# Graph layer on one Trainium2 core: the third kind's 256 edges multiplied directly in float32, a gather ring of eight slots, two of three tiles gathered plainly

## What is computed

```python
h = relu(layernorm(x))
feat = concat([h[src], h[dst]], axis=1)                 # 8192 x 2048
e_hh = relu(feat[:256] @ W_hh + b_hh)
e_oo = relu(feat[256:1536] @ W_oo + b_oo)
e_ho = relu(feat[1536:] @ W_ho + b_ho)
logit = concat([e_hh, e_oo, e_ho]) @ W_a + b_a          # one number per edge
alpha = softmax of logit over the edges of each dst
z = segment_sum(alpha[:, None] * h[src], dst)
x = x + relu([h, z] @ W_hn or W_on + bias)              # rows 0..127 W_hn, the others W_on
out = x + (normalised adjacency) @ (relu(layernorm(x)) @ W1.T + b1)
```

## Time and profile before

| | |
|---|---|
| median of 3 runs | 615.08 us |
| the profiled execution's own time | 616.7 us |
| its span in the profile | 614.9 us |
| TensorE busy | 559.2 us (91%) |
| VectorE busy | 446.3 us (73%) |
| ScalarE busy | 295.0 us (48%) |
| GpSimd busy | 183.1 us (30%) |
| DMA | 144.71 MB, mean 235 GB/s |

### The profile page before, as it was taken

The page is one execution under the profiler, slowest core; times in us unless marked ns, Lnnn a source line. Parts: engine busy times, 40 slices in busy tenths (PEclk is TensorE's granted clock), DMA queues, the critical chain, the costliest instruction groups (busy, mean ns, idle before and its releaser), DMA issues.

```text
span 614.9 us, 8170 instructions
## 1 busy us (share of the span) xinstructions
PE 559.2 (91%) x2360; PEld 409.3 (67%) x2361; DVE 446.3 (73%) x948; ACT 295.0 (48%) x471; POOL 183.1 (30%) x177
## 2 busy tenths in 40 slices
PE   1799999999796998898989987997998999999997
PEld 1688777777463676655657665564656887878885
DVE  6729157579596897899999967969547558888352
ACT  0723311122218989674857354958664445225200
POOL 3002110066355456445765466242000100000000
PEclk9899999999887999999998998789997899999999
DMA  8448774389999899999999999886864537502121
GB/s 324 156 148 287 245 266 154 110 194 374 346 310 319 268 322 313 341 290 331 373 354 345 304 334 336 271 216 166 284 214 128 191 92 250 186 0 86 52 86 51
DMA packets 56550, 144.71 MB, mean 235 GB/s; under 512 B 6338, under 2 KB 6466, under 8 KB 56514
## 3 DMA queue, kind: packets, MB, share of 16 engines
q0 software_dynamic: 22352, 81.28, 42.9%
q1 hardware_dynamic: 27072, 50.34, 24.2%
q10 hardware_dynamic: 7090, 12.65, 5.5%
HBM read 125.37 MB, written 18.87 MB: 235 GB/s over the span
## 4 chain that ended last, share of the span: by engine, by line
PE 47%; DVE 21%; DMA 15%; ACT 6%; issue 6%; POOL 3%; ACTq 1%; DVEq 0%; POOLq 0%
PE ps L710 29%; DMA gath<-tab_b,tabl_i 10%; PE ps L660 4%; PE ps L842 4%; PE ps L895 4%; DVE ring_l L970 4%; DVE gath L995 3%; ACT onehot L530 3%; PE ps L873 3%; DVE gath L990 2%; DMA gath<-tab_a,tabl_i 2%; DVE onehot L1011 2%; DMA tab_b<-stage 1%; DVE stage L978 1%; POOL gath L339 1%
## 5 line engine op out<-in xcount | busy, mean ns | idle before, releaser
L710 PE MATMUL ps<-ring_h,actT_h 128*128 128x512 f32 x504 | 218.9, 434 | 5.7 <-DVE actT_l L965 3.1
L710 PE MATMUL ps<-ring_h,actT_l 128*128 128x512 f32 x504 | 201.1, 399 | 0.0
L710 PE MATMUL ps<-ring_l,actT_h 128*128 128x512 f32 x504 | 200.8, 398 | 0.0
L530 ACT ACTIVATE onehot<-onehot,lgs 128x512 bf16<-128x512 bf16 x192 | 123.5, 712 | 64.1 <-DVE onehot L1011 57.5
L477 ACT CAST ring_h<-raw 128x512 fp32r<-128x512 f32 x160 | 94.9, 618 | 91.0 <-PE ps L710 68.7
L970 DVE TENSOR_TENSOR ring_l<-raw,ring_h 128x512 fp32r<-128x512 f32 x160 | 107.5, 687 | 27.0 <-ACT ring_h L477 26.6
L710 PEld LDWEIGHTS ps<-ring_h,actT_h 128*128 128x128 f32 x504 | 97.3, 193 | 38.8 <-DVE actT_l L965 3.3
L710 PEld LDWEIGHTS ps<-ring_h,actT_l 128*128 128x128 f32 x504 | 97.2, 193 | 22.0
L710 PEld LDWEIGHTS ps<-ring_l,actT_h 128*128 128x128 f32 x504 | 97.5, 193 | 19.9
L660 PE MATMUL ps<-onehot 128*128 128x512 bf16 x292 | 82.4, 393 | 27.1 <-ACT onehot L530 20.1
L995 DVE SCALAR_TENSOR_TENSOR gath<-gath,wa_b 128x1024 f32<-128x1024 f32 x64 | 78.4, 1225 | 27.6 <-DMA gath<-tab_b,tabl_i 25.6
(11 more groups left out here) (182 smaller groups left out, 539.2 us busy)
## 6 DMA issues: line engine op xcount, KB each, us to landing
raw<-in_L_gnn_W_ho_dram SPq DMA_DIRECT2D x32, 256.0 KB
raw<-in_L_gnn_W_oo_dram SPq DMA_DIRECT2D x32, 256.0 KB
raw<-in_L_gnn_W_hh_dram SPq DMA_DIRECT2D x32, 256.0 KB
raw<-in_L_gnn_W_on_dram SPq DMA_DIRECT2D x32, 256.0 KB
raw<-in_L_gnn_W_hn_dram SPq DMA_DIRECT2D x32, 256.0 KB
tab_a<-stage ACTq DMA_DIRECT2D x24, 256.0 KB
tab_b<-stage ACTq DMA_DIRECT2D x24, 256.0 KB
raw<-in_L_gnn_W_dram SPq DMA_DIRECT2D x16, 256.0 KB
```

The costliest lines, as they stand in the source:

```text
L530: ins = nc.scalar.mul(onehot[:, s, 1 + i, :], onehot[:, s, 1, :], lgs[:, i, q:q + 1])
L710: mm = nc.tensor.matmul(ps[:, first + m, :], w, v, start=(k == 0 and i == 0), stop=(k == KT - 1 and i == 2))
```

## The change

1. Kind hh gets no tables. Its 256 edges (2 tiles) are multiplied directly: GpSimd gathers the rows h[src] and h[dst] of both tiles from a stored copy `h_rows` (4 gathers), TensorE transposes them in chunk 1 (32 transposes of 128x128), ScalarE clips them at zero (8 operations), and the features of src stay in SBUF, those of dst are stored and loaded again (1 MB each way). The four hh chunks 8 to 11 become 16 float32 matmuls each, out of `raw` itself, with no rounding, no low part, no copies and no stores. VectorE adds the bias and takes the logits out of PSUM (`hh_edges`, 8 operations).
2. The ring has 8 slots in place of 10. Of the 62 tiles that are still gathered from tables, two of three are plain (41 plain, 21 accumulated); before it was 31 plain and 33 accumulated. The accumulating transfer is issued 2 tiles later in place of 3, and 5 tiles are begun ahead of `tab_b` in place of 6.
3. The order is written anew. Chunks 6 and 7 keep 7 tiles' sums each; the hh chunks have 5 sums and about 4 edges each; 12 and 13 have 7 and 5 sums. 16 of the 62 tiles and the 2 of hh are summed behind chunk 13, in two rounds "14" and "15" with no chunk under them; the first product of the node rows 0 to 127 stands among these, the second behind them. The kinds are closed in the order ho, hh, oo.
4. `inverse_counts` works on 1024 columns at a time in place of 256, and `hrow_l` is made a little earlier.

```diff
-        GB = 10
-        gath = sb("gath", [P, GB, D], F32, over="hrow", shift=8 * D)
+        GB = 8
+        gath = sb("gath", [P, GB, D], F32, over="hrow", shift=16 * D)
...
-        PLAIN = [q for q in range(T_HO + T_OO) if q % 2]
-        USES = [(q, e) for q in range(ET) for e in ((0, 1) if q in PLAIN else (0,))]
+        PLAIN = [q for q in range(TG) if q % 3]
+        USES = [(q, e) for q in range(TG) for e in ((0, 1) if q in PLAIN else (0,))]
...
+            def store_rows():
+
+                for m in range(NM):
+                    sp.wait_ge(s_norm, m + 1)
+                    sp.dma_start(h_rows[m * P:(m + 1) * P, :], hrow[:, m, :]).then_inc(s_hd, 16)
...
+            def load_behind_hh(w, row, n, c, k):
+
+                sp.wait_ge(s_slot, KT + (CH_HH + c) * KT + k + 1)
+                sp.dma_start(raw[:, k, :], w[row + k * P:row + (k + 1) * P, n * FB:(n + 1) * FB]).then_inc(s_raw[k], 16)
...
+            pool.wait_ge(s_hidx, 64)
+            pool.wait_ge(s_hd, 16 * NM)
+            for i in range(2 * T_HH):
+                pool.indirect_dma_start(out=hh_rows[:, i, :], out_offset=None, in_=h_rows[:, :],
+                                        in_offset=bass.IndirectOffsetOnAxis(ap=hh_i[:, i:i + 1], axis=0)).then_inc(s_hg[i], 16)
...
-            LAG = 3
-            FIRST = 6
+            LAG = 2
+            FIRST = 5
...
+        SUM_AT = {(6 + i, k): (i * 7 + k,) for i in range(2) for k in range(7)}
+        SUM_AT |= {(8 + i, k): (14 + i * 5 + j,) for i in range(4) for j, k in enumerate((0, 2, 3, 5, 6))}
+        SUM_AT |= {(12, k): (34 + k,) for k in range(7)}
+        SUM_AT |= {(13, k): (41 + k,) for k in range(5)}
+        SUM_AT |= {(14, 0): (46, 47), (14, 1): (48,), (14, 2): (49,), (14, 3): (50, 51), (14, 5): HH_TILES, (14, 6): (52, 53),
+                   (14, 7): (54, 55), (15, 0): (56, 57), (15, 1): (58, 59), (15, 2): (60,), (15, 3): (61,)}
...
+        EDGE_AT = {divmod(4 * KT + 4 + i // 7 * KT + i % 7, KT): (i,) for i in range(24)}
+        EDGE_AT |= {divmod(8 * KT + 2 * i, KT): (24 + i,) for i in range(16)}
+        EDGE_AT |= {(11, 7): (40,)}
+        EDGE_AT |= {divmod(12 * KT + (3 * i) // 2, KT): (41 + i,) for i in range(10)}
+        EDGE_AT |= {(14, 0): (51,), (14, 1): (52,), (14, 2): (53,), (14, 3): (54,), (14, 5): (55,), (14, 6): (56,), (14, 7): (57,),
+                    (15, 0): (58, 59), (15, 1): (60,), (15, 2): (61,)}
...
+            def hh_transposes(k):
+
+                for j in HH_AT.get(k, ()):
+                    if j == 0:
+                        for i in range(2 * T_HH):
+                            pe.wait_ge(s_hg[i], 16)
+                    if j >= 2:
+                        pe.wait_ge(s_ft, j - 1)
+                    for f in (2 * j, 2 * j + 1):
+                        for t in range(T_HH):
+                            c = f % 2 * E_HH + t * P
+                            mm = nc.tensor.transpose(ps[:, 2 + j % 2, c:c + P], hh_rows[:, 2 * t + f // KT, f % KT * P:(f % KT + 1) * P], ident[:, :])
+                    mm.then_inc(s_ftp, 1)
...
+            def hh_chunk(c):
+
+                half, n = HH[c]
+                for k in range(KT):
+                    sums(CH_HH + c, k)
+                    pe.wait_ge(s_raw[k], (CH_HH + c) * 16 + 16)
+                    if half and k == 0:
+                        pe.wait_ge(s_fld, 16)
+                    for t in range(T_HH):
+                        b = HH_BANK[n][t]
+                        if half == 0 and k == 0:
+                            pe.wait_ge(s_copied, NM * CH_HH + b - NM + 1)
+                        mm = nc.tensor.matmul(ps[:, b, :], featT[half][:, k, t * P:(t + 1) * P], raw[:, k, :],
+                                              start=(half == 0 and k == 0), stop=(half == 1 and k == KT - 1))
+                    mm.then_inc(s_slot, 1)
...
-            with pe.Fori(0, 6) as i:
-                edge_chunk(i + 6, before=lambda k: uniform_sums(i, k))
+            for q in (6, 7):
+                edge_chunk(q, before=lambda k: sums(q, k))
+            for c in range(4):
+                hh_chunk(c)
...
+            for k in range(4):
+                sums(14, k)
+            head_rows(0)
+            for c in (14, 15):
+                for k in range(4 if c == 14 else 0, KT):
+                    sums(c, k)
+            head_rows(1)
...
+            def hh_edges(n):
+
+                chunk_done(dve, CH_HH + 2 + n)
+                dve.wait_ge(s_bias, 48)
+                for t in range(T_HH):
+                    b = HH_BANK[n][t]
+                    c = slice(n * FB, (n + 1) * FB)
+                    step(nc.vector.tensor_tensor(ps[:, b, :], ps[:, b, :], bias2[:, 0, c], ALU.add))
+                    nc.vector.scalar_tensor_tensor(out=ps[:, b, :], in0=ps[:, b, :], scalar=0.0, in1=wa_b[:, c],
+                                                   op0=ALU.max, op1=ALU.mult, accum_out=lgh[:, t, n:n + 1]).then_inc(s_hhd, 1)
```

More of the change, by code:

```diff
@@ L170, in gnn_kernel @@
         s_root = sem("square_roots")
+        s_hd = sem("h_stored")
+        s_hidx = sem("hh_edges_loaded")
+        s_hg = [sem(f"hh_rows_gathered{i}") for i in range(2 * T_HH)]
+        s_ftp = sem("hh_transposed_banks")
+        s_ft = sem("hh_features_ready")
+        s_fst = sem("hh_dst_stored")
+        s_fld = sem("hh_dst_loaded")
+        s_hhd = sem("hh_banks_read")
         s_norm = sem("h_normed")
@@ L212, in gnn_kernel, with is_split, nth_split @@
         block = ctx.enter_context(nc.Block())
-        KINDS = ((W_ho, b_ho), (W_oo, b_oo), (W_hh, b_hh))
-        TILES = (T_HO, T_OO, T_HH)
-        CH_EDGE = 3 * 2 * NN
+        CH_HH = 2 * 2 * NN
+        CH_EDGE = CH_HH + 2 * NN
+        TG = T_HO + T_OO
+        HH = [(half, n) for half in range(2) for n in range(NN)]
+        HH_BANK = ((5, 6), (7, 4))
+        def is_split(q):
+            return not CH_HH <= q < CH_EDGE
+        def nth_split(q):
+            return q if q < CH_HH else q - (CH_EDGE - CH_HH)
         hn, on = (W_hn, (0,)), (W_on, (1, 2, 3))
@@ L221, in gnn_kernel @@
                 for r, order in ((0, ((on, 0), (on, 1))), (D, ((hn, 0), (hn, 1), (on, 0), (on, 1))))]
-        PLAIN = [q for q in range(T_HO + T_OO) if q % 2]
-        USES = [(q, e) for q in range(ET) for e in ((0, 1) if q in PLAIN else (0,))]
+        PLAIN = [q for q in range(TG) if q % 3]
+        USES = [(q, e) for q in range(TG) for e in ((0, 1) if q in PLAIN else (0,))]
         USE = {u: c for c, u in enumerate(USES)}
-        ADDED = {q: sum(1 for p in range(q + 1) if p not in PLAIN and USE[p, 0] % GB == USE[q, 0] % GB) for q in range(ET)}
+        ADDED = {q: sum(1 for p in range(q + 1) if p not in PLAIN and USE[p, 0] % GB == USE[q, 0] % GB) for q in range(TG)}
         def h_bank(k):
@@ L371, in _ @@
             bias(0, b_hh)
-            for q in range(FIRST, ET):
-                if q in (T_HO, T_HO + T_OO):
+            pool.wait_ge(s_ft, KT)
+            for q in range(FIRST, TG):
+                if q == T_HO:
                     tables_landed(kinds_of(q))
@@ L456, in _ @@
                     to += n
+            for e, end in enumerate((src, dst)):
+                for t in range(T_HH):
+                    act.dma_start(hh_i[:, 2 * t + e:2 * t + e + 1], end[t * P:(t + 1) * P].rearrange("(p a) -> p a", a=1)).then_inc(s_hidx, 16)
             def root(i):
@@ L570, in edge_chunk @@
                         seed(*SEED_AT[q, k])
-                    if k == 3 and 0 < q <= CH_EDGE and not is_a(q - 1):
+                    if k == 3 and 0 < q <= CH_HH and not is_a(q - 1):
                         store_b(q - 1)
@@ L588, in _ @@
             q = CH_EDGE + 2
-            keep_second_halves()
+            keep_second_halves((1,))
+            for at_ in SUM_AT:
+                if at_[0] >= q:
+                    for t in SUM_AT[at_]:
+                        logit_parts(t)
+            act.wait_ge(s_ohu, OS + 2 * ET)
+            keep_second_halves((2, 3))
             act.wait_ge(s_degin, 1)
@@ L1172, in top @@
             def top(m, n):
-                return topsum[:, m, n * FB:(n + 1) * FB] if m == 0 or n else stage[:, m - 1, :]
+                if m == 0 or m > 1 and n:
+                    return topsum[:, m, n * FB:(n + 1) * FB]
+                return stage[:, 3 if n else m - 1, :]
             def update_row(c, m):
```

257 lines of the change are left out of this document (151 added, 106 removed).

## The result

The changed kernel takes 628.7 us (median of 4, 627.7 to 634.3) against 614.9 for the kernel before beside it; the ratio is 1.025, 95% interval 1.020 to 1.031. I had said 603, with a range to 624. What came is rival B, which I had worked out at 629. The profiled execution took 628.2 us, its span is 626.4.

A forecast was written before the change was run, and what follows sets the result against it. No engine alone was taken to bound; the new ring's chain would set chunks 6 to 12. Chunk 6 to first exponential 19.4 us less, transposes 7.1 more: 616.7 - 12.3 = 604.4 profiled, 603 median, range 586 to 624.

The forecast's parts named there:

- rival B: Chunks 6 to 12 and tail: eight-slot ring too short, 5.3 us a tile, ending at 629 by the median; chance 0.20.
- start of chunk 6, against 187.2: Chunk 1: 32 added transposes at 0.222 us each on TensorE delay everything behind by 7.1 us.
- chunks 6 to 12: Logits of 36 tiles at 4.8 us each, 173 us.
- chunk 13: Goes by TensorE with four tiles only: 72 matmuls at 0.229 and five sums, 20.5 us.
- rounds 14 and 15, to the last one-hot: Behind chunk 13: 11 tiles by DMA or VectorE's work, both some 46, taken as 48 us for a float32 product.
- last one-hot to first exponential: Before the softmax: three ScalarE products 1.9, sum and closing 1.7, copies and root 4.0, together 7.6 us.
- behind the first exponential: Softmax and after: left as before; second product and loads of h's parts taken as covered.
- the pace: Chunks 6 to 12: a ring chain of 14.4 us for three tiles, 4.8 us a tile.
- L: In the ring chain: an accumulation from issue to landing, taken as 7.5 us, not the 11.58 of a full queue.
- the other links: Ring chain besides the landing: dst issue, gap, logits, add and other VectorE work, 6.9 us for three tiles.
- Rival A: Chunks 6 to 12 and tail: DMA binds, not the ring, 4.4 us a tile, 586 by the median; chance 0.22.
- Rival C: Behind chunk 13: TensorE idles, clock falls, round trip uncovered, 60 us in place of 48, total 615; chance 0.13.

The follow-up runs named there:

- before8: Kernel before with only the change's gather scheme (8 slots, two of three tiles plain, accumulation 2 tiles later, 5 begun early): 643.6 us, ratio 1.041.
- mid: Changed kernel with each accumulation issued between the src and dst gathers of a tile instead of behind both: 615.7 us, ratio 0.998.
- LAG 1: Accumulation issued one tile later: changed kernel (instead of two) 614.4 us; kernel before (instead of three) 626.1 us.
- beforelag1: Kernel before with the accumulation issued one tile later in place of three, nothing else: 626.1 us, ratio 1.019.
- half1tail: Changed kernel with every second tile plain, accumulation issued one tile later, and last sums reordered: 621.0 us, ratio 1.005.

## Why the prediction was wrong

The sum, against the profile of the changed kernel:

| term | said | measured | difference |
|---|---|---|---|
| start of chunk 6, against 187.2 | +7.1 | +1.5 | -5.6 |
| chunks 6 to 12 | 173 | 196.2 | +23.2 |
| chunk 13 | 20.5 | 21.4 | +0.9 |
| rounds 14 and 15, to the last one-hot | 48 | 49.5 | +1.5 |
| last one-hot to first exponential | 7.6 | 9.1 | +1.5 |
| behind the first exponential | 159.2 (as before) | 161.5 | +2.3 |

604.4 - 5.6 + 23.2 + 0.9 + 1.5 + 1.5 + 2.3 = 628.2, the profiled execution.

**The step that failed** is the pace, 4.8 us a tile. The mechanism was right, link for link, as before8 and mid show; two of its terms were sized too low. I took L, the accumulation from issue to landing, at 7.5 us, the lowest of two rows, "since a ring with fewer transfers out keeps the queue short". The ten accumulations on the chain between 157 and 358 us took 5.8 to 9.6, on average 8.0. And I took 6.9 us for the other links; between accumulations that follow each other on the chain there are 5.8 to 8.8 us, 7.5 on average over seven such gaps, the longer ones with another instruction of VectorE's order among them (1.1 + 1.2 us of the counts' inverses at 294.7). The seven loops that stand whole on the chain take 15.8 us for three tiles in place of 14.4, 5.26 a tile, past the point of 5.15 from which I had said it is a loss. The five in the two stretches where the chain runs over TensorE's order take 16.3 on average. What had seemed to confirm the reckoning was no check: (7 + 11.58)/4 = 4.6 took one row for the old ring, where only four accumulations of chunks 6 to 11 stand on the chain at all (10.0 to 11.6 us), at a DMA share of 0.99 to 1.03. So the old loop seldom bound, its L was no measure of the new one, and the 7.5 was chosen on an argument. Of the 23.2 us in the table some 18 are the pace, 36 tiles at 5.30 in place of 4.8; the other 5.3 are a 37th tile, which I had counted outside this stretch.

**Rival B** was therefore right in its place and in its pace (5.3 a tile), and had 0.20. That its total hit as well (630 by the profile, 628.2 came) is in part luck: it had 5.6 us too much for the transposes and 6.5 too much for the tail (56 against 49.5), and 5.2 too little for chunks 6 to 12 (191 against 196.2). **Rival A** could not be, as the loop stood above DMA's 4.4; in mid, without the loop, the pace was 4.84, so its 4.4 was not reached even then: the written order came next, with DMA at an estimated 4.65 close behind. By the Trainium skill, "DMA: Bandwidth & Descriptors", the section on the anatomy of a GpSimd-issued DMA, a landing would take an estimated 3.2 us; I gave that road to A. No accumulation on the changed kernel's chain landed in under 5.7 us, so the trace decides against it here.

**Rival C**, the naked tail, did not come. It had 60 us to the last one-hot in place of 48, and 49.5 were measured; VectorE is busy 39.3 of 53.5 us there, 73%. To the exponential there are 58.6 us against the 48 + 7.6 = 55.6 of my own sum, so the tail cost 3 us more, not 12. What it said of the clock is seen: 0.73 in that stretch. That the tail and the gathers take turns as its bound was not in any rival.

**The other signs.** Chunk 2 opens at 70.4, not 76: the transposes were another term mis-sized, in the other direction. Chunk 1 takes 3.6 us longer than before in place of 7.1; the other 2 us by which it opens early are chunk 0's, 22.0 us at a granted clock of 1.00 in this execution and 23.7 at 0.94 in that of the kernel before, and owe nothing to the change. The transposes stand in the stream of matmuls as

```profile
50.56 0.87 PE ps L879 x8
51.44 5.46 PE ps L811 x24
56.90 0.87 PE ps L879 x8
```

8 in 0.87 us, 0.109 each, 3.5 us for all 32. The row I took, 25 in 5.55 us, is of the first work TensorE does. The matmuls right behind it, from 22.93 us on in the kernel before, stand 0.43 us apart up to 25.6 and 0.23 after that, and the granted clock is 0.73 of 2.4 GHz from 20 to 25 us; so the row was probably of half speed, though the profile lists 1.00 from 10 to 20. The hh chunks took 87.4/4 = 21.9 us, above my 19 to 21; their matmuls are what I had said (in mid 8 records, four products, in 3.43 us, 0.86 each, against 0.88), so TensorE's 32 us are gained and go into the ring's pace, and without the loop the hh chunks take 20.2 each. The wait of 8.8 us for the hh tables is gone, GpSimd's waits for the logit are 148 us, where I had put B's sign at 150. The part behind the softmax I had left alone: 2.3 us more in this execution, 1.0 in mid's, not looked into.

## What to carry to other kernels

Where one engine issues a ring's transfers in a fixed order, write down behind which tile's completion and behind which landing each issue stands, and close both loops, in the old and in the new version; then see in the trace whether the old loop binds at all, before its latency is used. Here the scheme that shortens the distance from 3 to 2 cost the old kernel 28 us by itself and nothing in the busy shares warned of it. Swapping two issues on GpSimd gave back 13 us with the memory unchanged, and LAG 1 showed that earlier is not always better. And a break-even close to the forecast (5.15 against 4.8, 7%) asks for a range across it, not for a choice of the low end of a latency.

## What was not expected of the hardware

- The latency of these accumulations (128 rows of 4096 bytes) fell less than I had assumed: 10.0 to 11.6 us on the chain of the kernel before in chunks 6 to 11, at a DMA share of 0.99 to 1.03, and still 5.8 to 9.6, on average 8.0, in the changed kernel at 0.88 to 0.94.
- A wait for a landing in GpSimd's order holds up every gather behind it: 110.3 us in 28 waits at line 346 in beforelag1, 119.7 in 28 at line 410 in half1tail, some 4 us each. An accumulation must be issued late enough for its src rows and early enough for the ring.
- A float32 transpose of 128x128 in a stream of matmuls at full clock takes 0.109 us, half of what the row at the start of the kernel gave.
- In the rounds behind chunk 13, where TensorE has gaps, the granted clock is 0.73 of 2.4 GHz on average, between its two levels (1.2 and 2.4 GHz), and a sum takes 1.46 us in place of 0.82; in chunk 13, where TensorE is busy 20.35 of 21.40 us, it is 1.00. That may be a part of what moving sums under a chunk gives; no run parts it from the rest.
